# The ten value products of an attention layer move from the end of the key stage to between the scores of the attention's first three tiles

## The reference, cut to what matters

```
q = (x @ Wq + bq).reshape(B, S, NH, dh)
k = (x @ Wk + bk).reshape(B, S, NH, dh)
v = (x @ Wv + bv).reshape(B, S, NH, dh)
scores = jnp.einsum('bqhd,bkhd->bhqk', q, k) / jnp.sqrt(jnp.float32(dh)).astype(x.dtype)
attn = jax.nn.softmax(scores, axis=-1)
ctx = jnp.einsum('bhqk,bkhd->bqhd', attn, v).reshape(B, S, D)
sa = ctx @ Wo + bo
```

## Time and profile before

| | |
|---|---|
| median of 3 runs | 2299.52 us (2297.26 to 2300.3) |
| the profiled execution | 2299.0 us, of which the span from first to last instruction is 2297.3 us |
| PE busy | 2079.9 us, 91% of the span |
| DVE, ACT, POOL busy | 1352.2, 722.5, 378.3 us |
| key stage, from the first q unit | about 1632 to 1718 us |
| attention | about 1720 to 2143 us |
| experts | from about 2143 us to the end |

### The profile page before, as it was taken

How to read it: one execution, slowest core, us unless ns; L and a number is a source line. 1 busy time by engine, 2 the same in 40 slices (tenths; PEclk the granted TensorE clock), 3 DMA queues, 4 the chain that set the end, 5 groups by cost and what they waited for, 6 DMA issues and landing times. The chain is left out here.

```text
span 2297.3 us, 36539 instructions
## 1 busy us (share of the span) xinstructions
PE 2079.9 (91%) x13350; PEld 1819.2 (79%) x13351; DVE 1352.2 (59%) x3148; ACT 722.5 (31%) x1259; POOL 378.3 (16%) x314
## 2 busy tenths in 40 slices
PE   7976998899999999999999688999997999999586
PEld 5655665799989998998898668989877888888475
DVE  4544797344534444444467744565556878778667
ACT  3551101121221221212212322233335555555421
POOL 0000112000000000000000101111304444444444
PEclk9987999999999999999999999999998999999788
DMA  6651001121211211221101221111231021120542
GB/s 234 199 175 51 13 19 41 61 87 39 69 70 40 75 45 58 62 62 39 41 21 48 70 88 26 56 41 51 98 110 33 19 55 27 28 54 9 165 143 96
DMA packets 79283, 156.12 MB, mean 68 GB/s; under 512 B 7220, under 2 KB 22129, under 8 KB 77636
## 3 DMA queue, kind: packets, MB, share of 16 engines
q1 hardware_dynamic: 69584, 134.61, 19.4%
q0 software_dynamic: 4960, 11.49, 1.6%
q10 hardware_dynamic: 4616, 8.40, 1.0%
HBM read 104.15 MB, written 50.32 MB: 67 GB/s over the span
## 5 line engine op out<-in xcount | busy, mean ns | idle before, releaser
L130 PE MATMUL psum<-pt_hi,xn_hi 125*128 125x250 f32 x800 | 224.9, 281 | 3.3 <-DVE yt_lo L1123 1.6
L131 PE MATMUL psum<-pt_lo,xn_hi 125*128 125x250 f32 x800 | 223.7, 280 | 0.0
L132 PE MATMUL psum<-pt_hi,xn_lo 125*128 125x250 f32 x800 | 222.8, 278 | 0.0
L2360 POOL TENSOR_TENSOR mprob<-mprob,mrden 125x1250 f32<-125x1250 f32 x80 | 181.7, 2272 | 207.0 <-DVE mrden L2461 206.5
L131 PE MATMUL psum<-xt_lo,t_hi 128*125 128x512 f32 (+1 forms) x480 | 170.1, 354 | 0.0
L132 PE MATMUL psum<-xt_hi,t_lo 128*125 128x512 f32 (+1 forms) x480 | 169.8, 354 | 0.0
L130 PE MATMUL psum<-xt_hi,t_hi 128*125 128x512 f32 (+1 forms) x480 | 169.1, 352 | 0.0
L1061 ACT ACTIVATE prob<-prob,nb 125x1250 f32<-125x1250 f32 x40 | 53.7, 1342 | 354.4 <-DVE nb L1150 354.4
L2400 ACT ACTIVATE mprob<-psum,mbias 125x1250 f32<-125x1250 f32 x80 | 104.3, 1304 | 160.5 <-DVE mbias L2470 160.5
L2468 DVE TENSOR_REDUCE mmin<-psum 125x1 f32<-125x512 f32 (+1 forms) x240 | 127.1, 584 | 46.9 <-PE psum L2619 46.7
L130 PEld LDWEIGHTS psum<-pt_hi,xn_hi 125*128 125x128 f32 x800 | 151.2, 189 | 3.9 <-DVE yt_lo L1123 2.0
(11 more groups left out here) (504 smaller groups left out, 5841.4 us busy)
## 6 DMA issues: line engine op xcount, KB each, us to landing
slots_in<-slots_blank SPq DMA_DIRECT2D x12, 1282.5 KB, 11.1
cnt<-edge_counts SPq DMA_DIRECT2D x40, 305.2 KB
q_chunk<-q_store SPq DMA_DIRECT2D x40, 250.0 KB, 6.2
edge_attr<-in_attr SPq DMA_DIRECT2D x4, 1343.8 KB
slots_in<-slots_blank SPq DMA_DIRECT2D x3, 1539.0 KB, 18.5
moe_xg<-slots_in SPq DMA_DIRECT2D x17, 256.5 KB
raw_WqT<-in_WqT SPq DMA_DIRECT2D x4, 1024.0 KB, 7.8
raw_WkT<-in_WkT SPq DMA_DIRECT2D x4, 1024.0 KB
```

The source lines that it names most:

```text
L130: nc.tensor.matmul(out, lh, rh, start=start, stop=False)
L131: nc.tensor.matmul(out, lh, rl, start=False, stop=False)
L132: return nc.tensor.matmul(out, ll, rh, start=False, stop=stop)
L2360: nc.gpsimd.tensor_tensor(prob[:, n % 4, :], prob[:, n % 4, :], rden[:, n % 4:n % 4 + 1].broadcast_to([P, N]), ALU.mult).then_inc(p_ready, 1)
```

## The change

The ten value tiles leave the key stage: the units now end at `first_v`, for PE, ACT and DVE. The weights and the bias of the values are handed on (`g.wv`, `g.bv`, with the semaphore `g.bv_in` for the bias). In the attention's first chunk, steps 0, 1 and 2 get four, three and three value products (`VALUES`), which PE runs right behind the scores of the step, in banks 6 and 7, not used by the attention before step 5. Each step's ACT and DVE lists get the rounding of the same tiles. `v_sum` lies 256 bytes higher. SP's first load of the residual now waits for all ten sums, since it lands where the bias lies. ACT's wait for the stored q goes. PE waits for all ten low halves ahead of the first context product. The core of the diff (the removals of the same three loops' value branches are cut to one):

```diff
@@ -1978,23 +1971,13 @@
-            for u in range(total):
+            for u in range(first_v):
...
-                if u >= first_v:
-                    t = u - first_v
-                    if t == 0:
-                        dve.wait_ge(bv_in, 16)
-                    dve.wait_ge(done, u + 1)
-                    nc.vector.tensor_tensor(vsum[:, t % 2, :], kv_bank(u)[0:P, :], bv[:], ALU.add).then_inc(vs, 1)
-                    dve.wait_ge(hi, written(u + 1))
-                    nc.vector.tensor_tensor(g.v_lo[:, t, :], vsum[:, t % 2, :], f32(g.v_hi[:, t, :]),
-                                            ALU.subtract).then_inc(lo, 1)
-                    continue
...
+    vsum = at("v_sum", [P, 2, D], F32, 196.25)
+    v_done, v_summed, v_top, v_low = sem("v_done"), sem("v_summed"), sem("v_hi_done"), sem("v_lo_done")
+    VALUES = (range(0, 4), range(4, 7), range(7, NT))
+    value_bank = lambda t: core.bank(6 + t % 2)[0:P, :]
...
+            sp.wait_ge(v_summed, NT)
             residual_in(0)
...
                     if live(n):
                         exponentials(n)
+                    if n < len(VALUES) and isinstance(c, int) and c == 0:
+                        for t in VALUES[n]:
+                            act.wait_ge(v_summed, t + 1)
+                            nc.scalar.activation(g.v_hi[:, t, :], vsum[:, t % 2, :], ACT.Copy).then_inc(v_top, 1)
...
+            def value_sum(t):
+                if t == 0:
+                    dve.wait_ge(g.bv_in, 16)
+                if t >= 2:
+                    dve.wait_ge(v_low, t - 1)
+                dve.wait_ge(v_done, t + 1)
+                nc.vector.tensor_tensor(vsum[:, t % 2, :], value_bank(t), g.bv[:], ALU.add).then_inc(v_summed, 1)
+
+            def value_lo(t):
+                dve.wait_ge(v_top, t + 1)
+                nc.vector.tensor_tensor(g.v_lo[:, t, :], vsum[:, t % 2, :], f32(g.v_hi[:, t, :]), ALU.subtract).then_inc(v_low, 1)
...
                     if live(n):
                         maximum(n)
+                    if n < len(VALUES) and isinstance(c, int) and c == 0:
+                        for t in VALUES[n]:
+                            value_sum(t)
+                            if t:
+                                value_lo(t - 1)
+                            if t == NT - 1:
+                                value_lo(t)
...
+            def value(t):
+                if t >= 2:
+                    pe.wait_ge(v_summed, t - 1)
+                for k in range(KT):
+                    last = three_pass(nc, value_bank(t), [a[:, k, t * P:(t + 1) * P] for a in (g.xt_hi, g.xt_lo)],
+                                      [a[:, k, :] for a in g.wv], k == 0, k == KT - 1)
+                last.then_inc(v_done, 1)
...
                         scores(n)
+                    if n < len(VALUES) and isinstance(c, int) and c == 0:
+                        for t in VALUES[n]:
+                            value(t)
+                    if n == 5 and isinstance(c, int) and c == 0:
+                        pe.wait_ge(v_low, NT)
```

More of the change, by code:

```diff
@@ L1425, in dense_stages @@
     g.wo_raw = at("kv_raw", [128, KT, D], F32, 188)
-    vsum = at("v_sum", [P, 2, D], F32, 196)
-    bv, bo, beta2 = at("mha_bv", [P, D], F32, 4), at("mha_bo", [P, D], F32, 8), at("moe_beta2", [P, D], F32, 10)
+    g.wv = kv_hi[2], kv_lo[2]
+    g.bv = at("mha_bv", [P, D], F32, 4)
+    bo, beta2 = at("mha_bo", [P, D], F32, 8), at("moe_beta2", [P, D], F32, 10)
     bqk = at("mha_bqk", [128, 2, KT], F32, S + 1.21875)
@@ L1452, in dense_stages @@
     kv_in, kv_h, kv_l = [sem(f"kv_in{i}") for i in range(3)], sem("kv_hi_done"), sem("kv_lo_done")
-    kv_small, bv_in, q_bias = sem("kv_small_in"), sem("kv_bv_in"), sem("kv_q_bias")
-    done, hi, lo, vs = sem("kv_done"), sem("kv_out_hi"), sem("kv_out_lo"), sem("kv_vsum")
+    kv_small, q_bias = sem("kv_small_in"), sem("kv_q_bias")
+    done, hi, lo = sem("kv_done"), sem("kv_out_hi"), sem("kv_out_lo")
     q_stored = sem("kv_q_stored")
@@ L1473, in dense_stages @@
     first_k, first_v = len(units), 2 * len(units)
-    total = first_v + NT
     wide = [slice(0, 64), slice(64, 128)]
@@ L1492, in matrix @@
     def matrix(u):
-        return (u >= first_k) + (u >= first_v)
+        return int(u >= first_k)
     with nc.Block() as block:
@@ L1551, in _ @@
             sp.dma_start(kv_raw[2][:], kv_src[2]).then_inc(kv_in[2], 16)
-            sp.dma_start(bv[:], row_view(w["bv2"])).then_inc(bv_in, 16)
+            sp.dma_start(g.bv[:], row_view(w["bv2"])).then_inc(g.bv_in, 16)
             sp.wait_ge(g_out, 2 * NC)
@@ L1717, in _ @@
                     top(kv_hi[2], kv_raw[2], kv_in[2], kv_h, u - first_k + 8)
-                if u == first_v:
-                    act.wait_ge(q_stored, 32)
-                if u >= first_v:
-                    t = u - first_v
-                    act.wait_ge(vs, t + 1)
-                    nc.scalar.activation(g.v_hi[:, t, :], vsum[:, t % 2, :], ACT.Copy).then_inc(hi, 1)
-                    continue
                 m, a, b = units[u % first_k]
@@ L2162, in _ @@
             pe.wait_ge(g_added, NT)
-            for u in range(total):
+            for u in range(first_v):
                 j = matrix(u)
-                if u in (0, first_k, first_v):
+                if u in (0, first_k):
                     pe.wait_ge(kv_l, KT * j + KT)
@@ L2179, in _ @@
                 for k in range(KT):
[L2180 to L2189, removed]
+                    m, lo_, hi_ = units[u % first_k]
+                    last = three_pass(nc, kv_bank(u)[:, 0:hi_ - lo_],
+                                      [a[j][:, k, m * 128:(m + 1) * 128] for a in (kv_hi, kv_lo)],
+                                      [a[:, k, lo_:hi_] for a in (g.xt_hi, g.xt_lo)], k == 0, k == KT - 1)
                 last.then_inc(done, 1)
@@ L2936, in program @@
         g.wo_in = stack.enter_context(nc.semaphore("at_wo_in"))
+        g.bv_in = stack.enter_context(nc.semaphore("at_bv_in"))
         g.fc1_in = stack.enter_context(nc.semaphore("ffn_fc1_first_in"))
```

## The result

The changed kernel takes 2289.02 us (median of 5 runs, 2288.21 to 2290.37); the kernel before, 2299.79 (5 runs, 2297.26 to 2303.84). The ratio is 0.9952, 95% interval 0.9940 to 0.9964: 10.8 us less. The forecast was 2290.7, with a range of 2287.0 to 2296.0.

A forecast was written before the change was run, and what follows sets the result against it. It took the opening to be bound by the hand-over from DVE to ACT, PE elsewhere. 28.5 us earlier less 19.2 + 0.5 later gave 8.8 us off 2299.0, 2290.2; with 0.5 for the median, 2290.7, range 2287.0 to 2296.0.

The forecast's parts named there:

- What bounds: Attention opening: the hand-over from DVE to ACT sets 15.03 us; in value products and steady attention PE is the bound.
- Removed: 28.50 us: End of the key stage: without the value tiles there, the first scores start 28.50 us earlier.
- q in time, at nothing: Ahead of the first scores: the loaded q arrives in time, costing nothing, with a margin of 1.3 us.
- late-q rival: First scores: q loads land 3 us later than read, the opening slips about 1.7 us, 2292.4; chance 0.06.
- PE's work, 32.5 us: Ahead of the fourth tile's scores: three score groups, 120 value matmuls and one transpose group take 32.5 us at full clock.
- The clock, 1.7 us, once: Start of the opening: PE's clock falls after a 2.9 us rest, costing 1.7 us once; bounds 0 and 7.0.
- clock rival: Opening or steps 4 to 6: clock doesn't fall or falls less often, 1.7 to 3.4 us more gained; chance 0.13.
- slow-clock rival: Opening: PE stays at 1.2 GHz through the value products, making the kernel 22.0 us slower, 2321.5; chance 0.05.
- No wait on PE in there: Second, third and fourth scores: exponentials end before PE arrives, with slack of 8.6, 4.5 and 5.6 us.
- The tail, +0.5: After the last product: the fourth minimum waits behind value work in DVE's queue, adding 0.5 us; bounds 0 and 2.1.
- The sum: Whole kernel: 28.5 us earlier, 19.2 + 0.5 later, 8.8 us gained, forecast 2290.7; the shift should reach the end.
- the one fall that was allowed: Steps 4 to 6: one more or one fewer fall of the clock, each costing about 1.7 us.

The follow-up runs named there:

- all in one step: All ten value products put behind the first tile's scores, none behind the second and third, against the changed kernel's four, three, three; 2296.66 us.
- two-two-six: The same ten products placed two, two and six, against the changed kernel's four, three and three; 2291.26 us.
- both kernels with quarters: Changed kernel with the output weights' split cut into quarters: DVE in ACT's step, 2291.07 us, or one step behind, 2285.34 us.
- the repeat: The changed kernel measured again on another chip run, with no edit; 2291.10 us, ratio 0.9958 to the kernel before.
- the quarters that wait in order: Changed kernel with the output weights' split in quarters in steps 4 to 7, ACT and DVE in the same step; 2291.07 us.
- four moved: Six value tiles stay in the key stage and four move (two, one, one), against the changed kernel's ten moved; 2291.94 us.

## Why the prediction was right

- **What bounds.** Right. Its reading of the opening as a hole set by minimum, bias and exponentials is borne out by the kernel with all ten products in one place. There the wait for ACT is the one that PE shows.
- **Removed: 28.50 us.** Measured 28.16. The barrier distance was 1.41 for 1.42. The 0.35 between are upstream: the last k unit ended that much later in this execution. Counted from that unit, 28.51 us are removed.
- **q in time, at nothing.** Right: the first scores carry the same idle time and distance as the barrier alone explains. The late-q rival did not come.
- **PE's work, 32.5 us.** Measured 32.44 with the clock at 1.00.
- **The clock, 1.7 us, once.** Not borne out by the profile of the first result, where it held, and borne out by most others. Of seven profiles with a rest of 2.93 or 2.96 us (the changed kernel three times, all in one step, two-two-six, both kernels with quarters) the clock fell in five and held in two, the first of the changed kernel among these. Where it fell, S to fourth was 33.91 to 33.99: 1.5 more. So the forecast's term stands for most executions and was 0.2 too large. The first profile shows the course of the clock rival, whose 2287.3 to 2289.0 its median of 2289.02 touches; by these seven that rival should have had some 0.3 instead of 0.13. The slow-clock rival, products at 1.2 GHz for 20 us or more, never came, not even after 5.31 us of rest.
- **No wait on PE in there.** Right, and with about the margins named. The first exponentials end at 1697.12 (1695.81 + 1.31), 6.9 us before the second scores; 8.6 were reckoned, 1.7 of them for the clock. The second exponentials end at 1708.67 (1707.37 + 1.30), 4.9 us before the third scores; 4.5 were reckoned. The third end at 1718.18, 5.9 before the fourth; 5.6 were reckoned.
- **The tail, +0.5.** Measured 0.54, by the mechanism named: the minimum stands behind value work in DVE's queue. The transposes at 1727.91 name POOL, but POOL's scaling that ends there is of a later tile. The transposes are of the second tile, scaled from 1715.24 on; the piece at 1725.58 is the third's. What the banks wait for is DVE's first `ptm_lo`: it starts 0.81 us ahead of the transposes, as 0.82 before (1737.30 to 1738.12), and it stands behind the minimum.
- **The sum.** 28.16 - 17.41 - 0.54 = 10.21 against 8.8: the 1.4 between are the clock that held (1.7), less the 0.35 upstream. The forecast of 2290.7 was 1.7 us above the first median, 0.4 below that of the repeat and 2.9 above the third. That it came within 2 us of the first median is in part luck, since the term of the clock was wrong for that profile; where the clock fell, in the repeat, the fourth scores gain 9.55 us counted from the last k instruction, against 9.3 (28.5 less 19.2) in the forecast. That the shift reaches the end was right within the one fall that was allowed: 11.2 at the expert loads, 10.0 at the end.
- **A slip.** The prediction expects the first transposes about 34 us behind the first scores. Its own sum gives 33.0 (34.2 less the 1.17 of the transposes); measured are 31.43, with the clock held.

The Trainium skill, "TensorE: Matmul & The Clock Gate", section "What's actually happening", has the low clock as the default and lets activity raise it. The runs agree: after every fall here, with 2.93, 3.54 or 5.31 us of rest ahead, the clock was up again within the first products. Its section "Architectural detail" calls DVE's queue a strict first-in first-out one; the tail of 0.54 us and the quarters that wait in order (idle 2.11 and 1.88 us at 1734.07 and 1739.89) agree with it as well.

What stays open: how the gain divides between the idle time that was filled and the clock that it lifted, since no run changed one without the other; why the clock falls in some executions and not in others at the same rest, and from where the 7 us of spread ahead of the change come. No run aimed at any of the three.

## What to carry to other kernels

Moved work gains the room it fills, and little for leaving where it was (here 0.6 us, a shorter rest at the barrier): measure the holes first (here 10.5 us: 15.03 less the 4.5 of work at full clock that stays when the 27.9 of products are taken from 32.44), fill each just past the hand-over that sets it, and expect the rest of the work to bring next to nothing. Where a hole is filled, look at the queue of the engine that makes the next hand-over, since the new work stands in it too. A split that one engine begins and another ends belongs in two consecutive steps of the pipeline, not in one.

## What had not been expected

- Executions of the same kernel differ in when the same work ends, DVE's last k unit from 1686.15 to 1693.04 us over the profiles here. That is over half of the gain that was measured. A row's absolute time says nothing over two executions; short distances inside one agree to 0.1 us where the clock took the same course (33.91 to 33.99 in five profiles of four kernels). Over longer ones, falls of the clock at other places come in: from the fourth scores to the expert loads the changed kernel took 393.13, 393.60 and 393.77 us, two-two-six 395.31.
- After nearly the same rest (2.93 us, once 2.96), with the same work on either side, the clock fell in five profiles of seven. After 3.54 us (four moved) and 5.31 it fell as well, in one profile each. For four moved and two-two-six it fell only behind the first group of scores, which took 1.39 us as at full clock. A still shorter rest gives the same picture: after the 2.42 us ahead of the second transposes these took 1.41 us in the first profile of the changed kernel and 1.46 in two-two-six, but 2.43 or 2.44 in its second and third profile and in both kernels with quarters.
- The price of a fall was 1.5 us with 1.4 us of scores and dense products behind it, and 2.1 us after the rest of 5.31, in one profile.
